# Decoder layer with routed experts on one core: the router's logits products placed between the output projection's products

## What is computed

```
x = x + mixer(layernorm(x))
q, k, v = layernorm(x) @ wq.T + bq, ctx @ wk.T + bk, ctx @ wv.T + bv
x = x + (softmax(q k.T / 4) v) @ wo.T + bo          # output projection
h = layernorm(x)
logits = h @ Wg.T + bg                              # 16 per token
top_vals, top_idx = top_k(logits, 2)                # the router
x = x + sum over the two of softmax(top_vals) * expert[top_idx](h)
```

## Time and profile before

| | us |
|---|---|
| median of 3 executions | 640.2 (637.81 to 643.41) |
| the profiled execution, its own time | 636.72 |
| its span, first to last instruction | 634.9 |
| five passes, first logits product of the first to that of the fifth | 335.77 - 204.34 = 131.43 |
| mean granted TensorE clock, share of full speed | 0.948 |

### The profile page before, as it was taken

How to read it: one execution, slowest core, us unless ns; L and a number is a source line. 1 busy time by engine, 2 the same in 40 slices (tenths; PEclk the granted TensorE clock), 3 DMA queues, 4 the chain that set the end, 5 groups by cost and what they waited for, 6 DMA issues and landing times.

```text
span 634.9 us, 12808 instructions
## 1 busy us (share of the span) xinstructions
PE 527.1 (83%) x3216; PEld 297.1 (47%) x3217; DVE 486.2 (77%) x1349; ACT 331.9 (52%) x708; POOL 345.3 (54%) x447
## 2 busy tenths in 40 slices
PE   0895988958778899697979787999989999999960
PEld 0583824523334435252525242756545666556630
DVE  4677644794756867868787877898988778799997
ACT  3863582456668666666767623263323444444451
POOL 4759171072466586858686844255773343333445
PEclk9999897968999979989999997999999999999995
DMA  8922000006810010101010112345697444796756
GB/s 307 318 91 23 3 5 1 1 1 200 259 43 3 21 51 16 53 6 68 1 67 2 68 43 53 66 100 111 150 223 141 111 104 108 174 269 159 175 147 208
DMA packets 93678, 62.67 MB, mean 99 GB/s; under 512 B 68594, under 2 KB 78966, under 8 KB 93496
## 3 DMA queue, kind: packets, MB, share of 16 engines
q1 hardware_dynamic: 74232, 44.04, 26.7%
q0 software_dynamic: 6864, 16.86, 8.1%
q10 hardware_dynamic: 12528, 1.14, 2.1%
HBM read 27.97 MB, written 25.56 MB: 84 GB/s over the span
## 4 chain that ended last, share of the span: by engine, by line
PE 57%; DVE 23%; ACT 8%; issue 5%; POOL 3%; DMA 3%; DVEq 0%; ACTq 0%; SPq 0%; POOLq 0%
PE bank L1267 6%; PE bank L1081 5%; PE bank L1283 4%; PE bank L1408 4%; PE bank L1406 4%; PE bank L1405 4%; ACT AR L881 3%; DVE AR L1692 3%; DVE X L2042 3%; PE bank L1070 3%; PE bank L1415 2%; PE bank L1424 2%; PE bank L1297 2%; PE bank L1425 2%; PE bank L1427 2%
## 5 line engine op out<-in xcount | busy, mean ns | idle before, releaser
L737 POOL DMA_INDIRECT y_rows<-AR,CST x79 | 78.4, 992 | 117.4 <-ACT AR L981 89.4
L970 ACT ACTIVATE AR<-AR 128x256 f32<-128x256 f32 x79 | 32.9, 416 | 107.9 <-DVE AR L1957 102.8
L694 POOL DMA_INDIRECT xs_rows<-AR,SLOT x64 | 64.1, 1002 | 32.4 <-issue 20.0
L615 POOL TENSOR_TENSOR W<-STG,W 128x512 f16<-128x512 f32 (+1 forms) x48 | 55.4, 1159 | 47.3 <-ACT W L784 45.6
L1692 DVE RECIPROCAL AR<-bank 128x512 f32<-128x512 f32 x16 | 53.6, 3353 | 16.5 <-PE bank L1267 16.5
L881 ACT ACTIVATE AR<-bank 104x1024 f32<-104x1024 f32 (+1 forms) x48 | 48.4, 1022 | 32.0 <-PE bank L1251 32.0
L1680 DVE TENSOR_REDUCE MX<-bank 128x8 f32<-128x616 f32 x64 | 48.4, 793 | 16.1 <-PE bank L1216 15.8
L1964 DVE SCALAR_TENSOR_TENSOR AR<-AR 128x256 f32<-128x256 f32 x79 | 34.0, 430 | 14.0 <-ACT AR L970 12.2
L1267 PE MATMUL bank<-AR,VCUR 104*32 104x512 f32 (+1 forms) x256 | 36.6, 674 | 9.3 <-ACT AR L881 5.7
L782 ACT ACTIVATE STG<-W 128x512 f32<-128x512 f32 (+1 forms) x48 | 29.9, 623 | 22.4 <-POOL W L615 21.1
L1424 PE MATMUL bank<-W,AR 128*128 x158 | 39.8, 275 | 0.1
(11 more groups left out here) (259 smaller groups left out, 1406.6 us busy)
## 6 DMA issues: line engine op xcount, KB each, us to landing
W<-in_wexp SPq DMA_DIRECT2D x16, 768.0 KB, 5.5
AR<-y_rows SPq DMA_DIRECT2D x12, 512.0 KB, 4.6
X<-in_x SPq DMA_DIRECT2D x4, 1024.0 KB, 11.9
out<-X SPq DMA_DIRECT2D x16, 256.0 KB, 3.5
CST<-y_rows SPq DMA_DIRECT2D x4, 512.0 KB, 4.3
CST<-in_cst SPq DMA_DIRECT2D x1, 1309.0 KB, 8.4
CST<-xs_rows ACTq DMA_DIRECT2D x79, 1.0 KB
y_rows<-AR,CST POOLq DMA_INDIRECT x79
```

Of the source, the lines that this page charges most:

```text
L615: pool.tensor_tensor(w[:, 1], STG[:, q], w[:, 0], ALU.subtract).then_inc(s["w_split"], 1)
L694: pool.indirect_dma_start(xs_rows, bass.IndirectOffsetOnAxis(ap=SLOT[:, par, k, j:j + 1], axis=0), RB[:, par, j, :], None, bounds_check=XS ...
L737: pool.indirect_dma_start(y_rows, bass.IndirectOffsetOnAxis(ap=NIX[:, k:k + 1], axis=0), CY[:, k, :], None, bounds_check=TOPK * NTOK - 1, ...
```

## The change

In the five passes the eight logits products no longer stand in a row ahead of the eight of the output projection. A new function does both: for each of the four token tiles two logits products, then two products of the output projection. `lg_mm` is raised by the last logits product as before, which now has six products of the output projection ahead of it; `out_mm` is raised after the second and the fourth tile as before. The wait for `at_r`, which stood behind the logits, now stands ahead of them. First and last passes, and all other engines' programs, are as they were.

```
+            def out_and_logits(g):
+                pe.wait_ge(s["x3T_r"], 2 * (g - 1) + 2)
+                pe.wait_ge(s["at_r"], 2 * g + 2)
+                pe.wait_ge(s["x3T_r"], 2 * g)
+                for j in range(GT):
+                    for c in range(DC):
+                        lg = pe.matmul(route(g - 1)[0][:, j * NEXP:(j + 1) * NEXP], X3T[:, c, j * P:(j + 1) * P],
+                                       cst_w(C_WG, NEXP, c), start=(c == 0), stop=(c == DC - 1))
+                    if j == GT - 1:
+                        lg.then_inc(s["lg_mm"], 1)
+                    for c in range(DC):
+                        mm = pe.matmul(WK[j // 2][:, (j % 2) * D:(j % 2 + 1) * D], AT[:, c, j * P:(j + 1) * P],
+                                       cst_w(C_WO, D, c), start=(c == 0), stop=(c == DC - 1))
+                    if j % 2:
+                        mm.then_inc(s["out_mm"], 1)
...
                     if log:
                         pe.wait_ge(s["exp_r"], g * (2 * NCH) + 2)
-                        s3_logits(g - 2)
-                    if out:
+                        out_and_logits(g - 1)
+                    elif out:
                         s2_out(g - 1)
                     s1_turn(g + 1)
```

## The result

| | before | after |
|---|---|---|
| median of 4 executions each, us | 639.49 (637.81 to 643.41) | 648.35 (647.36 to 650.1) |
| ratio, 95% interval | | 1.0146 (1.0103 to 1.0189) |
| profiled execution, its time and its span, us | 636.72, 634.9 | 648.62, 646.8 |
| mean granted clock of it | 0.948 | 0.945 |
| first logits product of the first pass to that of the fifth, us | 131.43 | 344.32 - 204.29 = 140.03 |

The changed kernel is slower by 1.5%, and the interval is clear of 1. The two profiled executions differ by 11.90 us: the way from the first to the fifth pass grew by 8.60, the way behind it by 3.35, and the first pass began 0.05 earlier.

The account below looks back on a forecast made before the run. PE's eight products, with DVE's router hidden under them, were taken to set the time after the logits. 636.72 + 9.5 + 1.0 + 1.0 = 648.2 us; on the median 651.7, less one clock fall 650.0; range 641 to 658.

Parts of the forecast that it names:

- The step: PE to DVE: router starts 2.66 us later, no longer hidden, transposes at 8.68 instead of 6.44; 2.24 us a pass.
- The third pass: PE's low clock after its logits was expected to go with mixing, so this pass costs only 0.58 us.
- POOL's string: ACT's weight pieces and POOL's splits move by 2.66 us, 0.42 more than DVE's; 0 to 2.1 in all, 1.0 taken.
- The clock after the gap: PE idles 3.2 us before the transposes; clock falls in most passes, mostly hidden; 0.2 a pass, 1.0 us in all.
- Loads do not hide: Denies the rival that logits weight loads hide under PE's output projection: + 1.5, 641.7 us from the median; chance 0.15.
- The clock rival: Each PE gap brings a long clock fall without cover before MH: 8 us more, 658; chance 0.12.
- Faster: Mixing removes a low clock after logits in all five passes and loads hide: 5.2 us gained, 635.0; chance 0.08.
- The sum for the profiled execution: Whole kernel: 636.72 + 9.5 + 1.0 + 1.0 = 648.2 us.
- the first two terms: Five passes: 9.5 us for the later router and transposes, plus 1.0 for ACT's and POOL's work ahead of the scatter.
- one fall of the clock behind the logits: PE's low clock after the logits, which the change might remove: 1.67 us off the median's 651.7, giving 650.0.

Follow-up runs that it names:

- The late signal alone: Kernel before, all logits first, but `lg_mm` raised only by the sixth product of the output projection: 650.78 us, ratio 1.0187.
- two products late: Kernel before, all logits first, but `lg_mm` raised only by the second product of the output projection: 646.74 us, ratio 1.0139.
- the wait alone: Kernel before with only the wait for `at_r` put ahead of the logits in the five passes: 637.09 us, ratio 0.998.
- before with the weights moved: Kernel before, ACT's router exponential put behind its weight pieces and DVE's three router-weight instructions behind the maxima: 638.37 us, ratio 1.0005.
- the additions first: Changed kernel with DVE's two additions of the output projection put ahead of the router in the five passes: 662.5 us, ratio 1.0369.
- the weight pieces early: Changed kernel with ACT's wait for the router moved behind its three weight pieces, so POOL's splits need not wait: 651.75 us, ratio 1.0224.
- The filled gap: Changed kernel with six products whose result nothing reads put between output projection and transposes: 651.48 us, ratio 1.0174.
- the logits two tiles ahead: Changed kernel with only two output projection products ahead of the last logits: 647.2 us, ratio 1.0149; once more, 645.75 us.
- wait moved back: Kernel with two products ahead of the last logits, its wait for `at_r` put behind the first four logits products: 641.53 us, ratio 1.0038.

## Why the prediction was right

- **The step.** It was to be a `lg_mm` that is late by six products, which ends the hiding of the router under PE's products. The late signal alone gives the whole loss, and two products late a part of it. The router's start was put at 4.66 and stands at 4.57 to 4.60 in all five passes; the transposes were put at 8.68 and stand at 8.41 to 8.74; PE's gap was put at 3.2 and is 2.9 to 3.2; DVE's longest wait for the logits was put at 5.1 and is 5.1; ACT's L909 was put 2.7 later and is 2.57 later; first to fifth was put at about +9 and is +8.60.
- **The third pass** was to lose only 0.58, since its row no longer runs at a low clock. Its transposes went from 8.11 to 8.74, 0.63. The fall after the logits is indeed gone from it, but that the mix removed it is not shown: in the four other profiles with all logits in a row (the wait alone, both late signals, before with the weights moved) the clock did not fall there in any pass, so it fell in 1 of 25. That the profiled execution had it was chance, and the price of 0.58 holds for this execution alone.
- **POOL's string** was priced as a surcharge of 1.0, between 0 and 2.1, on a step of 9.5 by way of the transposes. The sum of the scatter's shifts, 10.85, agrees with 10.5, but the runs show the weights the other way round: the string is the path and the transposes are not (the additions first). That neither string has slack, as the prediction said, was wrong for PE's; its price came out near because both strings follow the router's 2.6 us. DVE's slots are close behind POOL's string: freed of the splits, the scatter came only 0.50 and 0.35 us earlier (the weight pieces early, second and fourth pass). POOL's string also reaches DVE. In the fourth pass the slots ended later by 2.5 and not by the additions' 2.06 because a product of 128x4 elements (L1799 above) was held until POOL's third split ended, 321.87 and 321.86; before, the same instruction was held less:

```profile
312.74 0.59 DVE L1783 TENSOR_TENSOR RW<-RD,RW 128x4 f32 x1
```

  It ended at 313.33 with the split of the earlier trace rows at 313.31. Where it is free it takes 0.16.
- **The clock after the gap** was expected to fall in most passes and to be hidden for the most part, at 0.2 a pass. It fell in four of five, and in the third 0.73 of the rest of the pass shows; the others show nothing. The filled gap bears this out: with the clock restored, the first pass is as long as with it low, and the third gets its 0.7 back.
- **The rivals.** Loads do not hide: 32 mixed instructions take the 5.5 us that the two rows took. The clock rival falls with the filled gap. Faster falls with the result.
- **The level.** The sum for the profiled execution was 648.2, and it took 648.62; by the parts it is 10.6 at the start of the expert stage, which is the 9.5 + 1.0 of the first two terms, then 1.05 less within that stage and 2.40 more by the last DMA, and neither of these two was foreseen. That the sum comes within 0.4 us is therefore luck in part: its 1.0 for the clock was too much, and the last DMA made up for it. For the median the text started from 640.2 and took off one fall of the clock behind the logits, 1.67, to reach 650.0; the medians differ by 8.86, so 11.5 - 8.86 = 2.6 was to be taken off. The reason that was given has no support, since such a fall was the exception (1 of 25 passes); that a term of this size was right to take off is luck. The profiled execution of before, 636.72, was faster than the four of its median, and its last DMA was 2.40 us shorter than the changed kernel's. That is as large as the term that was wanted; that it is the reason is not shown, since executions without a profile do not show that DMA.

## What to carry to other kernels

When products are reordered on PE, ask first who waits for the last of them and what that engine has yet to do behind the wait: an early semaphore hides that work, and a mix that spreads the products evenly brings it into the open at no gain on PE. Before pricing a shift, find the string that sets the length of a pass, by a distance that stays the same from pass to pass and from version to version (here first split to scatter, 7.3 us, and scatter to the next logits, 19.4 to 19.6), and price the change by where it meets that string. Such a distance holds only as long as nothing else ends later: with the scatter 1 us earlier than before it became 20.1 to 21.6. And where executions of one kernel differ by their mean granted clock, compare versions within one such group, else a step of 3 us reads as 9.

## What was not expected of the hardware

- Some tiny DVE instructions were held for as long as a 128x512 f32 `tensor_tensor` of POOL ran, until its end: 0.17 became 1.13 for a copy of four elements a partition, 0.16 became 1.04 for a product, and a `tensor_scalar` of four elements took 2.19 beside two splits. The earlier trace rows had shown it of MH alone. Not all are held: in the first pass with the weight pieces early, the maxima (four in 0.41 us) and the index searches (0.16 each) took beside the same split what they take without it. Moving POOL's work thus moves time on DVE, as the early weight pieces did by up to 1.5 us a pass.
- The same 3.00 us of idle time on PE was followed by a low clock in the second pass and not in the fourth, in both profiles of the changed kernel.
- One indirect DMA at the end of 79 on POOL took over 3 us where most take 0.97: the last in twelve profiles, the last but one in one, none in before. Between the profiles of before and after it moved the end of the span by 2.4.
- Executions of one kernel on the same chip had mean granted clocks near 0.945 or near 0.935, in before on each of three chips. Which falls make the difference was seen only where an execution of the lower group was profiled, above all in the kernel with the logits two tiles ahead and in its variant with the wait moved back (two falls of some 10 us, at 2.3 us each); what decides for the one or the other is open.
